# Stepping an attention loop in pairs: one block of scores and numerators for two steps

## The reference

```python
def _favor_plus(x, W):
    sq = 0.5 * jnp.sum(x * x, axis=-1, keepdims=True)
    return jnp.exp(x @ W - sq) * INV_SQRT_NF
...
def step(carry, qkv):
    S, z = carry
    q_t, k_t, v_t = qkv
    S = S + jnp.einsum('bhd,bhe->bhde', k_t, v_t)
    z = z + k_t
    num = jnp.einsum('bhd,bhde->bhe', q_t, S)
    den = jnp.einsum('bhd,bhd->bh', q_t, z) + EPS
    return ((S, z), num / den[..., None])
...
q, k, v = (heads(Wq), heads(Wk), heads(Wv))
qp = _favor_plus(q, W_feat)
kp = _favor_plus(k, W_feat)
y = _causal_linear_attention(qp, kp, v)
```

## Time and profile before

| what | us |
|---|---|
| median of 3 runs | 252.59 (252.52 to 252.64) |
| the profiled execution, its own time | 252.84 |
| its span | 251.0 |
| PE busy | 240.3 (96% of the span) |
| DVE busy | 187.2 (75%) |
| ACT busy | 146.6 (58%) |
| POOL busy | 101.6 (40%) |
| first P of step 1 to first P of step 15 | 80.32 to 177.58 |

### The profile page before, as it was taken

How to read it: one execution, slowest core, us unless ns; L and a number is a source line. 1 busy time by engine, 2 the same in 40 slices (tenths; PEclk the granted TensorE clock), 3 DMA queues, 4 the chain that set the end, 5 groups by cost and what they waited for, 6 DMA issues and landing times.

```text
span 251.0 us, 7011 instructions
## 1 busy us (share of the span) xinstructions
PE 240.3 (96%) x2736; PEld 189.2 (75%) x2736; DVE 187.2 (75%) x474; ACT 146.6 (58%) x285; POOL 101.6 (40%) x139
## 2 busy tenths in 40 slices
PE   8998889999999999999999999999999999999985
PEld 7854557777687778777777787777788988888845
DVE  5677888666733585867888888775578999999985
ACT  0553453544445788567556666755747257787772
POOL 2073113342202558443673568727530034444430
PEclk9999999999999999999999999999999999999999
DMA  6999999991079001100110000000000000000002
GB/s 179 367 384 404 396 396 394 340 393 45 1 224 331 33 0 46 44 3 1 44 44 3 1 3 3 3 0 3 4 3 3 4 0 3 21 21 24 22 24 65
DMA packets 15521, 26.83 MB, mean 107 GB/s; under 512 B 1248, under 2 KB 8832, under 8 KB 15488
## 3 DMA queue, kind: packets, MB, share of 16 engines
q1 hardware_dynamic: 14720, 25.96, 29.1%
q10 hardware_dynamic: 768, 0.43, 0.6%
HBM read 25.33 MB, written 1.05 MB: 105 GB/s over the span
## 4 chain that ended last, share of the span: by engine, by line
PE 62%; DVE 14%; DMA 5%; SPq 5%; POOL 5%; issue 4%; ACT 4%; DVEq 0%; POOLq 0%; ACTq 0%
PE b L1364 11%; PE b L1124 8%; PE b L1126 7%; PE b L1125 7%; PE b L1408 6%; DMA wv_raw<-in_aWv 5%; PE b L1383 4%; PE b L1285 3%; PE b L1288 2%; PE b L1495 2%; PE b L1281 2%; SPq L270 2%; PE b L1536 2%; SPq L276 2%; DVE yT_lo L996 1%
## 5 line engine op out<-in xcount | busy, mean ns | idle before, releaser
L868 DVE TENSOR_TENSOR x_lo<-b,x_hi 128x512 fp32r<-128x512 f32 x32 | 21.7, 688 | 16.8 <-ACT x_hi L472 16.7
L609 ACT ACTIVATE phi<-b 128x512 f32<-128x512 f32 x48 | 26.0, 597 | 11.3 <-PE b L1364 11.3
L354 POOL TENSOR_TENSOR lnr<-lnv,mh 128x1 f32<-128x1 f32 x16 | 8.8, 551 | 55.6 <-DVE lnv L732 55.6
L412 POOL TENSOR_TENSOR sq_lo<-sq_sum,sq_hi 128x512 fp32r<-128x512 f32 x16 | 20.6, 1286 | 25.8 <-ACT sq_hi L472 25.8
L530 ACT ACTIVATE sq<-b 128x512 f32<-128x512 f32 x32 | 19.3, 603 | 18.2 <-PE b L1126 18.2
L406 POOL TENSOR_TENSOR sq_sum<-sq,sq 128x512 f32<-128x512 f32 x16 | 20.7, 1294 | 21.7 <-ACT sq L530 21.7
L1124 PE MATMUL b<-nT_lo,wp_hi 128*128 128x512 f32 x64 | 26.8, 419 | 0.1
L1126 PE MATMUL b<-nT_hi,wp_hi 128*128 128x512 f32 x64 | 25.1, 392 | 0.0
L1125 PE MATMUL b<-nT_hi,wp_lo 128*128 128x512 f32 x64 | 25.0, 391 | 0.0
L942 DVE TENSOR_TENSOR smk<-b,mask 64x512 f32<-64x512 f32 x32 | 22.0, 688 | 2.9 <-PE b L1383 1.2
L1408 PEld LDWEIGHTS b<-va,smk 128*64 128x64 f32 x512 | 17.5, 137 | 7.4 <-issue 7.0
(11 more groups left out here) (181 smaller groups left out, 617.9 us busy)
## 6 DMA issues: line engine op xcount, KB each, us to landing
cT<-in_ctxT SPq DMA_DIRECT2D x8, 1028.0 KB, 14.2
cn<-in_ctx SPq DMA_DIRECT2D x8, 1024.0 KB, 14.9
wv_raw<-in_aWv SPq DMA_DIRECT2D x1, 1024.0 KB, 13.7
wp_raw<-in_aWq SPq DMA_DIRECT2D x4, 256.0 KB, 4.7
wp_raw<-in_aWk SPq DMA_DIRECT2D x4, 256.0 KB, 4.7
w_raw<-in_w2T SPq DMA_DIRECT2D x1, 1024.0 KB, 5.6
wo<-in_aWo SPq DMA_DIRECT2D x1, 1024.0 KB, 8.1
w_raw<-in_w1T SPq DMA_DIRECT2D x1, 1024.0 KB, 5.0
```

Source lines behind the costliest of these rows:

```text
L412: nc.gpsimd.tensor_tensor(sq_lo[n % 2][:], sq_sum[:], sq_hi[n % 2][:].bitcast(F32), ALU.subtract).then_inc(sq_l, 1)
L609: nc.scalar.activation(phi(n, a)[:], feature_bank(a), ACT.Exp).then_inc(f_exp, 1)
L868: nc.vector.tensor_tensor(x_lo[n % 2][r][:], proj_bank(n, r), x_hi[n % 2][r][:].bitcast(F32), ALU.subtract).then_inc(x_l, 1)
```

## The change

Steps 3 to 14 go in pairs (n odd, j = (n-3)/2). PE does P of n, P of n+1, E of n-1, one block `group(j)` = N, A, N, A, N, N (heads 4j-2 to 4j+1, scores 2j and 2j+1), then E of n. P of even steps goes to b6 and b7, P of odd steps to b0 and b1; scores go to b0 and b1, numerators to b0, b6, b6, b7 in turn. x_hi and x_lo have three buffers instead of two. ACT, DVE and POOL are put in the same order: ACT takes all four `squares` of a pair one after another; DVE has one `quantise_w` between the `low` of n and of n+1 and, up to n = 9, a second one at the end. POOL splits quad 1's first half before step 2 instead of 3; wo is split in its high part after step 10 (four casts) and in its low part after steps 13 and 14. SP loads w1 first, w2 after the last transposed group, and wo after all quads, into the place that w1's raw weights had. Steps 1, 2 and 15 stay single. The work is the same.

```diff
@@ banks
-            return (b5, b7)[r] if n == 0 else (b0, b1)[r][:]
+            return (b5, b7)[r] if n == 0 else ((b6, b7)[r], (b0, b1)[r][:])[n % 2]
...
-            return {13: b0[:], 14: b2[:], 15: b4}.get(u, b6)
+            return {12: b6, 13: b0[:], 14: b2[:], 15: b4}.get(u, (b0, b1)[u % 2][:])
...
+            return late.get(v, (b0[:], b6, b6, b7)[v % 4] if v < 22 else b7)[:, 0:HALF * VW]
@@ SP
+            sp.dma_start(w1_raw[:], w1T.rearrange("(c p) n -> p c n", p=P)).then_inc(ld_w1, 16)
+            sp.wait_ge(nT_mm, NG)
             sp.dma_start(w2_raw[:], w2T.rearrange("(c p) n -> p c n", p=P)).then_inc(ld_w2, 16)
-            sp.dma_start(wo[:], aWo.rearrange("(c p) n -> p c n", p=P)).then_inc(ld_wo, 16)
...
+            sp.wait_ge(w_quant, 4)
+            sp.dma_start(wo[:], aWo.rearrange("(c p) n -> p c n", p=P)).then_inc(ld_wo, 16)
@@ POOL
             for n in range(STEPS):
-                if n % 4 == 3 and n < STEPS - 1:
+                if n == 2:
+                    split_quad(1, 0)
+                if n % 4 == 3 and 3 < n < STEPS - 1:
                     split_quad(n // 4 + 1, 0)
...
-                if n in (9, 10, 13, 14):
-                    split_wo((9, 10, 13, 14).index(n))
+                if n == 10:
+                    split_wo_high()
+                if n == 13:
+                    split_wo_low(0)
+                    split_wo_low(1)
+                if n == 14:
+                    split_wo_low(2)
+                    split_wo_low(3)
@@ ACT
+            for n in range(3, STEPS - 1, 2):
+                if n > 3:
+                    features(n - 2, 0, 1, 2, 3)
+                squares(n, 0)
+                squares(n, 1)
+                squares(n + 1, 0)
+                squares(n + 1, 1)
+                squares_high(n)
+                features(n - 1, 0, 1, 2, 3)
+                squares_high(n + 1)
@@ DVE
+            for n in range(3, STEPS - 1, 2):
+                j = (n - 3) // 2
+                low(n, 0)
+                low(n, 1)
                 if 5 <= n < 13:
-                    quantise_w(n - 5)
+                    quantise_w(n - 4)
+                low(n + 1, 0)
+                low(n + 1, 1)
+                if j >= 1:
+                    outputs(4 * j - 2)
+                masked(2 * j)
+                if j >= 1:
+                    outputs(4 * j - 1)
+                else:
+                    weight_scales()
+                outputs(4 * j)
+                masked(2 * j + 1)
+                outputs(4 * j + 1)
+                if n < 11:
+                    quantise_w(n - 3)
@@ PE, waits of project(n, r)
-                    if n >= 2:
-                        pe.wait_ge(sq_f, 2 * (n - 1) + r + 1)
-                        pe.wait_ge(x_l, 2 * (n - 1) + r + 1)
+                    if n >= 3:
+                        pe.wait_ge(sq_f, 2 * (n - 2) + r + 1)
+                        pe.wait_ge(x_l, 2 * (n - 2) + r + 1)
+                    if n >= 5 and n % 2 == 1 and r == 0:
+                        pe.wait_ge(n_y, 2 * (n - 5) + 1)
+                    if n >= 5 and n % 2 == 1 and r == 1:
+                        pe.wait_ge(s_mask, 2 * (n - 4) + 2)
+                    if n >= 6 and n % 2 == 0:
+                        pe.wait_ge(n_y, 2 * (n - 6) + 2)
@@ PE, waits of numerators(v), beside s_mask of its own scores
+                elif v == 1 or (v < 22 and v % 4 >= 2):
+                    step, r = 2 * ((v + 2) // 4) + 4, 1 if v % 4 == 3 else 0
+                    pe.wait_ge(sq_f, 2 * step + r + 1)
+                    pe.wait_ge(x_l, 2 * step + r + 1)
+                elif v < 22 and v % 4 == 1:
+                    pe.wait_ge(n_y, v - 2)
@@ PE, the order
+            def group(j):
+                if j >= 1:
+                    numerators(4 * j - 2)
+                attention(2 * j)
+                if j >= 1:
+                    numerators(4 * j - 1)
...
+                attention(2 * j + 1)
+                numerators(4 * j)
+                numerators(4 * j + 1)
...
+            for n in range(3, STEPS - 1, 2):
                 project(n, 0, 1)
+                project(n + 1, 0, 1)
                 exponents(n - 1)
+                group((n - 3) // 2)
+                exponents(n)
```

More of the change, by code:

```diff
@@ L115, in build @@
         y = z.take("y", [P, NG, E])
-        wo = z.take("wo", [P, HC, D])
+        x_hi2 = [z.take(f"x_hi2{r}", [P, TOK], F32R) for r in range(2)]
+        x_lo2 = [z.take(f"x_lo2{r}", [P, TOK], F32R) for r in range(2)]
         wo_hi = z.take("wo_hi", [P, HC, D], F32R)
@@ L127, in build @@
         phi_23.append([[z2.take(f"phi_b{t}{a}", [P, TOK]) for a in range(2, QUAD)] for t in range(2)])
-        w2_raw = z2.take("w2_raw", [P, HC, D])
+        x_hi.append(x_hi2)
+        x_lo.append(x_lo2)
+        wo = Region(z2.at).take("wo", [P, HC, D])
+        w1_raw = z2.take("w1_raw", [P, DC, HID])
         smk = [z2.take(f"smk{h}", [P, 2 * HALF, P // PT, PT]) for h in range(2)]
         wo_lo = Region(z2.at).take("wo_lo", [P, HC, D], F32R)
-        w1_raw = z2.take("w1_raw", [P, DC, HID])
+        w2_raw = z2.take("w2_raw", [P, HC, D])
         z = Region(work_at)
@@ L413, in squares_low, with split_wo_high, split_wo_low @@
                                         ALU.subtract).then_inc(sq_l, 1)
-            def split_wo(k):
-                if k == 0:
[L417 to L421, removed]
+            def split_wo_high():
+                pool.wait_ge(ld_wo, 16)
+                for k in range(4):
+                    at = slice(2 * k, 2 * k + 2)
+                    nc.gpsimd.tensor_copy(wo_hi[:, at], wo[:, at]).then_inc(wo_split, 1)
+            def split_wo_low(k):
+                at = slice(2 * k, 2 * k + 2)
+                if k == 0:
+                    pool.wait_ge(w_quant, 8)
+                    pool.wait_ge(wo_split, 4)
                 nc.gpsimd.tensor_tensor(wo_lo[:, at], wo[:, at], wo_hi[:, at].bitcast(F32),
@@ L530, in squares @@
                 nc.scalar.activation(sq[r][:], proj_bank(n, r), ACT.Square).then_inc(sq_f, 1)
[L531 to L533 removed]
+                if n >= 3:
+                    act.wait_ge(f_mm, 4 * (n - 3) + 4)
+                copy(x_hi[n % 3][r][:], proj_bank(n, r)).then_inc(x_h, 1)
             def squares_high(n):
@@ L611, in _ @@
             squares_high(0)
-            for n in range(1, STEPS):
+            for n in (1, 2):
                 squares(n, 0)
@@ L617, in _ @@
                 features(n - 1, 2, 3)
+            for n in range(3, STEPS - 1, 2):
[8 more added lines that the diff above has]
+                squares_high(n + 1)
+            features(STEPS - 3, 0, 1, 2, 3)
+            squares(STEPS - 1, 0)
+            squares(STEPS - 1, 1)
+            features(STEPS - 2, 0, 1)
+            squares_high(STEPS - 1)
+            features(STEPS - 2, 2, 3)
             features(STEPS - 1, 0, 1, 2, 3)
@@ L865, in low @@
                 dve.wait_ge(x_h, 2 * n + r + 1)
-                if n >= 2:
-                    dve.wait_ge(f_mm, 4 * (n - 2) + 4)
-                nc.vector.tensor_tensor(x_lo[n % 2][r][:], proj_bank(n, r), x_hi[n % 2][r][:].bitcast(F32),
+                if n >= 3:
+                    dve.wait_ge(f_mm, 4 * (n - 3) + 4)
+                nc.vector.tensor_tensor(x_lo[n % 3][r][:], proj_bank(n, r), x_hi[n % 3][r][:].bitcast(F32),
                                         ALU.subtract).then_inc(x_l, 1)
@@ L967, in outputs @@
                     ALU.mult).then_inc(n_y, 1)
-            for n in range(1, STEPS):
+            for n in (1, 2):
                 low(n, 0)
-                if n == 4:
-                    weight_scales()
                 low(n, 1)
@@ L976, in _ @@
                     clear_scores()
+                    weight_sum(0, w1_raw[:], ld_w1)
+                else:
                     weight_sum(1, w2_raw[:], ld_w2)
[L978 to L988, removed]
-                if 5 <= n < 13:
-                    quantise_w(n - 5)
+            for n in range(3, STEPS - 1, 2):
+                j = (n - 3) // 2
+                low(n, 0)
+                low(n, 1)
+                if 5 <= n < 13:
+                    quantise_w(n - 4)
[6 more added lines that the diff above has]
+                    outputs(4 * j - 1)
+                else:
+                    weight_scales()
[4 more added lines that the diff above has]
+                    quantise_w(n - 3)
+            low(STEPS - 1, 0)
+            low(STEPS - 1, 1)
+            outputs(22)
+            masked(12)
+            masked(13)
+            outputs(23)
             def yTc(g, c):
@@ L1353, in exponents @@
             def exponents(n):
-                h, order = n % 2, head_order(n)
+                h, x, order = n % 2, n % 3, head_order(n)
                 pe.wait_ge(x_l, 2 * n + 2)
                 pe.wait_ge(sq_l, n + 1)
-                terms = [(w[:, r], v[h][r]) for w, v in ((feat_hi, x_hi), (feat_lo, x_hi), (feat_hi, x_lo))
```

(36 more changed lines are left out.)

13 lines of the change are left out of this document (8 added, 5 removed).

## The result

The changed kernel takes **249.78 us** (median of 4 runs, 249.37 to 249.94) against 252.56 (252.24 to 252.64) for the kernel before on the same chip: ratio 0.9887, 95% interval [0.9864, 0.9909]. The prediction was 249.5, range 248.8 to 251.3. The profiled execution took 249.94 with a span of 248.1 us; before it was 252.84 with 251.0.

The account below looks back on a forecast made before the run. PE's instruction list was taken to bound the loop. Five pairs save 3.29, the start saves 0.3 and POOL loses 0.5, 3.1 us saved: 249.5 us against the median, range 248.8 to 251.3.

Parts of the forecast that it names:

- P in one run, block in one run: PE's order in a pair of steps: start-to-start times sum to 13.73 us without waits, where two steps took 14.67.
- rival B: Pair tighter than counted, DVE or ACT late in most pairs, or switches inside the block cost 0.2; saves 0.5 to 2.6; chance 0.30.
- The mask wait: Before head 4j, PE waits 0.28 us once per pair for DVE's mask of scores 2j, making a pair 14.01.
- The wait for y: Inside the block, the 0.27 us PE lost per step until DVE emptied the shared numerator bank goes.
- x_lo before head 4j-2: x_lo of step n+1 is ready at 7.1 us of the pair, PE comes at 7.75: 0.64 to spare.
- the upper bound of 2.6: DVE's quantising ahead of x_lo meeting POOL in full would cost 2.6 us at most; 0 was taken.
- The start: Steps 1 to 4: P of step 3 no longer waits for x_lo, step 5 starts near 103.9 instead of 104.24; 0.3 saved.
- POOL before P of step 12: Casts of wo before quad 3's split make POOL late for P of step 12; 0.5 us lost, bounds 0 and 1.0.
- The sum: Whole kernel: 3.29 + 0.3 - 0.5 = 3.1 us saved, 249.7 for the profiled execution, 249.5 against the median.
- The low end of the range: Whole kernel with no POOL wait and half the mask wait: 3.7 to 3.9 saved, 248.8 us.
- C: Slower: ACT's Squares of n+1 wait for POOL's late sum of n; 253.8 to 258.8 us; chance 0.05.
- D: No change, waits only move, needing 0.6 us of new waits in every pair; 252.6; chance 0.05.

Follow-up runs that it names:

- the shifted block: The changed kernel with each block starting one head earlier, at head 4j-3 (N, A, N, N, A, N); measured 248.82 us.
- with the casts: The changed kernel with blocks starting one head earlier and the four casts of wo moved from after step 10 to after step 12; measured 248.14 us.

## Why the prediction held

- **P in one run, block in one run.** Forecast 13.73 without waits; measured 14.01 - 0.28 = 13.73. The pieces agree to 0.02. With the mask wait really gone, in the shifted block, it is 13.67: the row from which N, N to E was priced at 1.08 itself stood behind a mask and holds 0.05 of its cost. Of the 0.66 that a pair gained, 0.26 is waiting (0.54 before, 0.28 after), and 0.40 is left for the changes of form; adding one visit back to N cost 0.13, and one back to P 0.23, together 0.36. The switches between N and A that a part of rival B priced at 0.2 cost nothing, and N to E no more than in the rows.
- **The mask wait.** Forecast 0.28 in each pair, from A's start plus 1.15 plus 1.41; measured 0.28 in all five, and taken away by moving one head.
- **The wait for y.** Forecast gone, and gone. But the run that put it back for the second head shows that this was no saving by itself: the 0.54 of two waits before became the 0.28 of one, set by the mask.
- **x_lo before head 4j-2.** Forecast 0.64 to spare; measured 0.64. It holds only as E stands in front of the block: without it, 0.70 is lost each time. The quantising before it took 0.52 and 0.75, so the upper bound of 2.6 for its meeting with POOL (by its own terms 4 x 0.71, 2.8) stayed unused. A quantising at another place did meet POOL: the one at 104.41 began 0.23 behind sq_lo and took 1.35, and no row of PE waited for it. The instructions that read PSUM keep their 0.69, as x_lo at 122.02 beside POOL's sum of 121.57 to 122.85. By the rule of the Trainium skill (GPSIMD Engine Reference, Specifications) that was weighed before, those that read PSUM are untouched; the trace agrees.
- **The start.** Forecast 0.3, measured 0.31. What the prediction took for granted there, the sooner split, is worth 2.3 us of wait, and 4 with the clock's fall.
- **POOL before P of step 12.** This is the term that was mis-sized. The prediction took 0.5 between 0 and 1.0; it is 0.78. The count to sq_lo was right (12.5). The casts beside DVE took 0.65 more than alone, just as in the row of before (1.40); with that taken in full the same sum gives 16.95 + 0.65 - 16.87 = 0.73, and the slower start of P after a stop, 0.11, stood in no term.
- **The sum.** Forecast 249.7 for the profiled execution (252.84 - 3.1); it was 249.94. POOL's term is 0.28 too small, the sooner start of step 2 (0.13) was not forecast, and the other terms differ by 0.05 in all. The low end of the range was added up wrongly: no POOL wait and half the mask wait is 3.29 + 0.3 + 0.7, 4.3 saved and 248.3, not 3.7 to 3.9 and 248.8. The measured 249.78 lies well above both.
- **Rivals.** C needed POOL late in all pairs: it is late in one, and its lateness there is the split and not the sum of squares. D needed new waits of 0.6 per pair: there are 0.28, already counted. B's waits appear only when P is put apart.

## What to carry to other kernels

On an engine that is busy all the time, a list of start-to-start times per block, with a price for each change of form, gave the time of a pair in the new order to a few hundredths, because each wait was followed to what is late next: removing one wait is worth only what lies between it and the next. The two forecasts that missed by 1 us, the shifted block alone and with the casts, took the gain of one block for that of every block. When work is moved closer together, look at every piece of side work on a slow engine that was due "one step later" and is now due at once; here two such places were worth 0.8 us and 4 us, one kept and one avoided by the change. Small gains can be blocked by each other and should be tried together.

## What the runs showed of the hardware beyond this

- 2.1 us without a matmul inside a stretch at full clock were followed by a stretch (95.5 to 98.9) at a granted clock of 0.50, with P's matmuls 0.43 apart instead of 0.23. That is the one traced execution; six of the other nine have the same mean clock of 0.993 and about the same time, and three stayed at 1.00. Idle stretches of 0.48 us (before P of step 12) and 0.84 us (the same place with the shifted block) had no such after-effect.
- Two equal casts on POOL take 0.74 alone and 1.39 while DVE quantises from SBUF, whose own two instructions took 0.49 and 0.76, no longer than alone. Where DVE's first instruction started 0.1 to 0.2 behind a subtraction of POOL's, it was DVE that took longer (1.47, and 1.35 at 104.41 of the changed kernel). In these meetings the one that came second paid. It is not a rule without exception: in the kernel before, at 157.11, DVE began 0.2 behind POOL's two casts, kept its 0.48, and the casts took 0.94.
- After a wait, the first matmul of P is followed by the next after 0.34 instead of 0.23, even without a change of form (149.34 in the changed kernel, 148.00 with the shifted block).
